# One Sign for two steps of a ternary weight, two row sums on another engine, and a new order of the preparation

## The reference, cut to what matters

```
x1 = x  + g * attention(layernorm(x), context)        Wq, Wkv, Wout; 8 heads, 128 context rows
x2 = x1 + g * W_proj' relu(W_fc' n + low-rank(n))^2   W' = ternary values times a scale per row
x3 = x2 + g * (Wx n + Wc mean(context) + b)           one matrix (512, 1024), split in two
x4 = x3 + g * (w2' q(gelu(w1' q(n) + b1)) + b2)       w' = ternary values times one scale; q: 8 bits
```

## Time and profile before

| what | value |
|---|---|
| runs, us | 1144.89, 1142.49, 1146.16 (median 1144.89) |
| the profiled execution's own time | 1145.46 |
| its span, first to last instruction | 1143.4 |
| TensorE, matmuls | busy 1086.2 (95%) |
| VectorE | busy 923.9 (81%) |
| ScalarE | busy 798.3 (70%) |
| POOL | busy 584.6 (51%) |
| mean granted clock of TensorE | 0.980 |
| moved by DMA | 128.11 MB |

### The profile page before, as it was taken

How to read it: one execution, slowest core, us unless ns; L and a number is a source line. 1 busy time by engine, 2 the same in 40 slices (tenths; PEclk the granted TensorE clock), 3 DMA queues, 4 the chain that set the end, 5 groups by cost and what they waited for, 6 DMA issues and landing times.

```text
span 1143.4 us, 22172 instructions
## 1 busy us (share of the span) xinstructions
PE 1086.2 (95%) x8270; PEld 676.6 (59%) x8558; DVE 923.9 (81%) x1989; ACT 798.3 (70%) x1575; POOL 584.6 (51%) x567
## 2 busy tenths in 40 slices
PE   5776799999999999999999999999999999999997
PEld 5544556475756656474756656565756666564744
DVE  3786788988788797878889888888878777988676
ACT  3988957677685949485876849495775868595634
POOL 1442646564655655556546457463546466564421
PEclk9988799999999999999999999999999999999998
DMA  9779751452534443433335245334343254333110
GB/s 335 239 241 317 232 147 41 95 130 65 120 79 103 98 105 86 100 82 87 93 83 139 61 112 97 86 101 87 89 99 99 54 109 114 75 93 74 38 47 28
DMA packets 273802, 128.11 MB, mean 112 GB/s; under 512 B 247568, under 2 KB 248080, under 8 KB 272016
## 3 DMA queue, kind: packets, MB, share of 16 engines
q1 hardware_dynamic: 273136, 125.73, 43.6%
q10 hardware_dynamic: 560, 0.96, 0.3%
HBM read 57.19 MB, written 8.39 MB: 57 GB/s over the span
## 4 chain that ended last, share of the span: by engine, by line
PE 86%; DMA 4%; ACT 3%; DVE 3%; issue 1%; SPq 1%; POOL 1%; ACTq 0%; DVEq 0%
PE ps L1844 19%; PE ps L1818 18%; PE ps L1887 10%; PE ps L1903 9%; PE ps L1866 7%; PE ps L1771 6%; PE ps L1718 6%; PE ps L1824 2%; PE ps L1758 2%; PE ps L1743 2%; DMA w1T<-in_wcT 1%; PE ps L1611 1%; DMA hT<-q 1%; PE ps L1683 1%; PE ps L1660 1%
## 5 line engine op out<-in xcount | busy, mean ns | idle before, releaser
L1818 PE MATMUL ps<-xT,fcT 128*128 128x256 f16 x2048 | 259.1, 274 | 8.2 <-DMA xT<-x16f 3.9
L732 POOL TENSOR_TENSOR rs<-ve,nhalf 128x1 f32<-128x1 f32 x160 | 102.1, 643 | 283.1 <-DVE ve L1357 207.9
L1844 PE MATMUL ps<-pjT,hid 128*128 128x512 fp8e4 x1024 | 232.1, 379 | 0.0
L1818 PEld LDWEIGHTS ps<-xT,fcT 128*128 128x128 fp8e4 x2048 | 199.1, 98 | 47.1 <-issue 6.5
L759 POOL TENSOR_TENSOR hid<-sq,hid 128x512 f16<-128x512 f32 x128 | 158.6, 1246 | 49.8 <-ACT sq L996 49.3
L1844 PEld LDWEIGHTS ps<-pjT,hid 128*128 128x128 f16 x1024 | 98.3, 98 | 98.9
L949 ACT ACTIVATE e<-ps,nmb,sig 128x128 f32<-128x128 f32 x256 | 113.0, 458 | 7.9 <-DVE nmb L1395 7.8
L985 ACT ACTIVATE rl<-ps,rsf 128x256 f32<-128x256 f32 x256 | 106.5, 469 | 15.6 <-PE ps L1824 14.9
L1887 PE MATMUL ps<-w1T,q4T 128*128 128x512 fp8e4 x480 | 113.4, 379 | 0.0
L764 POOL TENSOR_TENSOR e<-e,einv 128x512 f32<-128x512 f32 x64 | 71.0, 1116 | 74.2 <-DVE einv L1399 73.9
L1903 PE MATMUL ps<-w2T,hT 128*128 128x512 fp8e4 x480 | 108.6, 379 | 0.3 <-DMA hT<-q 0.3
(11 more groups left out here) (243 smaller groups left out, 1987.6 us busy)
## 6 DMA issues: line engine op xcount, KB each, us to landing
xb<-in_x SPq DMA_DIRECT2D x16, 512.0 KB, 4.3
xa<-in_x SPq DMA_DIRECT2D x15, 512.0 KB, 3.9
out<-r SPq DMA_DIRECT2D x30, 256.0 KB, 2.3
rope<-in_rope SPq DMA_DIRECT2D x16, 384.0 KB, 3.5
h<-in_w1T SPq DMA_DIRECT2D x6, 1024.0 KB, 6.4
h<-in_w2T SPq DMA_DIRECT2D x6, 1024.0 KB, 5.9
hid<-in_w_fc SPq DMA_DIRECT2D x2, 1024.0 KB, 8.7
h<-in_wkvT SPq DMA_DIRECT2D x2, 1024.0 KB, 10.3
```

The source lines that it names most:

```text
L732: pool.tensor_tensor(rs[:, n, t:t + 1], ve[:, n, t:t + 1], nhalf[:, :], ALU.pow).then_inc(done, 1)
L1818: pe.matmul(ps[:, FFN0 + m % 2, a * G:(a + 1) * G], fcT[:, k, f * P:(f + 1) * P], xT2[:, xs, k, :], start=(xs == 0 and k == 0), stop=False)
L1844: mm = pe.matmul(ps[:, FFN0 + t, :], hid[:, xs, c, t * P:(t + 1) * P], pjT[:, c, :], start=(c == 0 and xs == 0), stop=(c == FC - 1 and xs ...
```

## The change

1. The lift and the clip of w1 and w2 become one ScalarE operation, Sign with bias -MAGIC, from the rounded piece straight to fp8 in w1T or w2T. The clips, their two buffers and the constant go; c_tern12 counts in the place of c_lift and c_clip. The waits for the free destination (wc used for w1T, wx's two halves made for w2T) move from VectorE to ScalarE.
2. `ROWS_ACT = 2`: the row sums of w_fc's pieces 2 and 3 are made by VectorE, one reduce over (4, 512) each, inside "thr 2" and "thr 3".
3. ORDER and PREP are set anew. In groups 2 to 15 the positions shift, and the sequences on each engine differ from before by an operation passing a few neighbours, some of them in nearly every group. In the preparation and the first two groups they differ by more, as below.

```diff
+        ROWS_ACT = 2
...
-                dve.wait_ge(c_rows, KC * (i + 1))
...
+                if q < ROWS_ACT:
                     dve.wait_ge(c_rows, KC * (i + 1))
                 else:
-                    sc, cols = scd[:, i:i + 1], slice(FC + i, FC + i + 1)
                     arrived(dve, q)
-                    dve.tensor_reduce(sc, piece[PLACE[q]], axis=AX.X, op=ALU.add, apply_absolute_value=True).then_inc(c_rowd, 1)
-                    dve.wait_ge(c_rowd, i + 1)
+                    dve.tensor_reduce(sc, src, axis=AX.X, op=ALU.add, apply_absolute_value=True).then_inc(c_rowd, 1)
+                    dve.wait_ge(c_rowd, q - ROWS_ACT + 1)
...
                     act.wait_ge(c_round, n + 1)
-                    if n >= 2:
-                        act.wait_ge(c_clip, n - 1)
-                    else:
-                        used(act, last_in(4))
-                    act.activation(lifted[n % 2], piece[PLACE[W0 + n]], ACT.Relu, bias=lift[:, :]).then_inc(c_lift, 1)
+                    act.activation(dst, piece[PLACE[W0 + n]], ACT.Sign, bias=drop[:, :], saturate=False).then_inc(c_tern12, 1)
...
-            def clip_weights(n):
...
                 if first(g) and u == 0:
-                    pe.wait_ge(c_clip, 4)
+                    pe.wait_ge(c_tern12, 4)
```

More of the change, by code:

```diff
@@ L241, in build @@
         ktmp = rl[:, :, :]
-        lifted = [hT[:, t, :, :].rearrange("p c n -> p (c n)").bitcast(BF16) for t in range(TILES)]
         vT_sb = small[:, 0:KC * RANK].rearrange("p (k r) -> p k r", k=KC)
@@ L529, in build @@
-        PREP = dict(
-            PE=dict(x3_turn=(632, 634), q4_turn=(638, 642), q5_turn=(648, 649, 650, 651, 653, 654, 655, 656),
-                    k=(2, 3), v=(5, 6), low=(0,), mix=(14,), tern=(4, 9, 11, 16, 18, 19, 20, 21), low_t=(23,),
-                    row_scale=(27,), mean=(30,), spread=(1, 10, 12, 15, 26)),
-            DVE=dict(x3lo_end=(814, 817), ctx_sum=(14,), rot_k=(8, 9), wq_max=(4,), wq_scale=(5,), k_max=(16,),
-                     wq_lo=(7,), v_max=(17,), kv_scale=(23,), k_lo=(27,), v_lo=(31, 36), low_copy=(22,),
-                     thr=(6, 13, 18, 34, 44, 45, 47, 48), wo_max=(20,), v_top=(24,), wo_scale=(25,), wo_lo=(29,),
-                     mix_row=(51,), low_rank=(39,), v_parts=(52,), wx_max=(50,), hidden=(55,), wx_scale=(67,),
-                     wx_lo=(88,), row_scale=(62,), mean=(70,), diag=(56,), round=(72, 73, 81, 86, 90, 91, 98, 102),
-                     clip=(76, 80, 87, 92, 94, 97, 114, 129)),
-            ACT=dict(q4_end=(549, 550), wq=(5,), k_hi=(18,), v_hi=(20, 21), tanh=(1,), wo=(19,),
-                     evac=(7, 14, 16, 30, 34, 35, 36, 37), rows=(4, 8, 10, 22), whole=(6, 11, 13, 29), low=(42,),
-                     wx=(53,), sums=(39, 40, 41, 44, 45, 46, 47, 49), lift=(55, 56, 64, 67, 74, 79, 81, 83)),
-            POOL=dict(whole=(19, 20, 21, 22), rot_k=(7, 8), csb=(13,), low_zero=(14,)),
-            SP=dict(u=(1,), rows=(15,), ctx=(0,), wk=(4,), wq=(2,), wv=(7,),
-                    piece=(3, 5, 9, 16, 14, 22, 21, 18, 26, 28, 30, 31, 32, 35, 36, 37, 38, 39, 43, 44, 46, 49, 52, 55),
-                    wo=(8,), wc=(20,), wx=(19,), b1=(45,)))
@@ new lines, in build @@
+                pv=((17, 22), (47, 52), (84, 87), (122, 123), (160, 162), (198, 201), (237, 241), (272, 278),
+                    (314, 316), (354, 357), (395, 396), (434, 435), (466, 475), (511, 515), (549, 553), (588, 592)),
+                wo=((24, 25), (54, 55), (89, 90), (125, 126), (166, 167), (203, 204), (243, 244), (282, 283),
+                    (319, 320), (359, 360), (399, 400), (438, 439), (478, 479), (518, 519), (557, 558), (594, 595)),
+                low=((33,), (60,), (95,), (133,), (174,), (211,), (251,), (289,), (330,), (370,), (408,), (447,),
+                     (486,), (524,), (564,), (603,)),
@@ new lines, in build @@
+        PREP = dict(
+            PE=dict(x3_turn=(632, 634), q4_turn=(638, 641), q5_turn=(648, 649, 650, 651, 653, 654, 655, 656),
+                    k=(1, 2), v=(6, 7), low=(12,), mix=(14,), tern=(4, 8, 10, 16, 18, 19, 20, 21), low_t=(23,),
+                    row_scale=(26,), mean=(30,), spread=(0, 9, 11, 15, 29)),
+            DVE=dict(x3lo_end=(806, 808), ctx_sum=(6,), rot_k=(7, 10), wq_max=(0,), wq_scale=(3,), k_max=(19,),
+                     wq_lo=(8,), v_max=(20,), kv_scale=(23,), k_lo=(26,), v_lo=(28, 32), low_copy=(29,),
+                     thr=(9, 16, 17, 38, 44, 45, 46, 48), wo_max=(21,), v_top=(22,), wo_scale=(24,), wo_lo=(30,),
+                     mix_row=(50,), low_rank=(40,), v_parts=(70,), wx_max=(55,), hidden=(51,), wx_scale=(66,),
+                     wx_lo=(81,), row_scale=(63,), mean=(68,), diag=(52,), round=(69, 73, 78, 83, 86, 87, 93, 107)),
+            ACT=dict(q4_end=(547, 548), wq=(4,), k_hi=(16,), v_hi=(17, 20), tanh=(1,), wo=(19,),
+                     evac=(7, 13, 14, 28, 32, 33, 34, 35), rows=(5, 8), whole=(6, 11, 12, 27), low=(38,), wx=(50,),
+                     sums=(37, 39, 40, 41, 42, 45, 46, 49), lift=(52, 57, 61, 66, 70, 79, 83, 87)),
+            POOL=dict(whole=(19, 20, 21, 22), rot_k=(6, 7), csb=(9,), low_zero=(14,)),
+            SP=dict(u=(3,), rows=(25,), ctx=(0,), wk=(2,), wq=(1,), wv=(5,),
+                    piece=(4, 9, 11, 16, 18, 13, 17, 21, 26, 27, 31, 30, 34, 35, 36, 37, 38, 41, 42, 43, 44, 49, 50, 56),
+                    wo=(12,), wc=(14,), wx=(20,), b1=(45,)))
@@ L1287, in prepare @@
                     dve.tensor_copy(lowsb, lowprod).then_inc(c_low, 1)
-                for n in here("DVE", "clip", p):
-                    clip_weights(n)
                 for n in here("DVE", "round", p):
```

286 lines of the change are left out of this document (140 added, 146 removed), and 126 rows, old and new, of tables (down, exp, h, hid).

## The result

The changed kernel takes **1150.3 us** (median of 6 runs, 1147.53 to 1151.52), the kernel before 1145.21 in the same session (6 runs): the ratio is 1.0050, 95% interval 1.0037 to 1.0063. It is slower by half a per cent, 5.7 us by the ratio. The forecast was 1140.4, with a range up to 1145.5; the slower rival, C, had been given 0.07 and a mechanism that did not come about. Later comparisons are given as ratios to the kernel before in the same session, which there had medians of 1143.92 to 1144.72; 0.1% is 1.1 us.

A forecast was written before the change was run, and what follows sets the result against it. The preparation before TensorE's dense part at about 145 us was taken as the bound; the profiled 1145.46 less 4.5 gave 1141.0, and the median of runs, 0.57 lower, 1140.4 us, with a range of 1134.5 to 1145.5.

The forecast's parts named there:

- Rival C: Slower: VectorE's reduce delays low_rank, spread 3 and later ternary pieces; 2.5 to 4.5 us lost, 1147 to 1149; chance 0.07.
- (1) Eight clips: Eight clips leave VectorE, 13.1 us; first needed far behind 145 us, so worth nothing alone, only freeing VectorE's queue.
- Later orders: Orders behind the first groups differ by swaps of neighbours under a dense TensorE: 0, with 1.5 us either way.
- The walk: Step-by-step forecast of the preparation up to group 1's output projection, 4 to 4.5 us gained by then.
- Start: wq issued 0.5 us earlier, low-rank product no longer first: K starts at 14.2 us, before at 17.71.
- The low-rank product: Moved behind ternary piece 2, priced at 6.98 us, running to 52; scores then start at 52.4, 0.9 us gained.
- The mix: After group 0's scores: with the gap filled it costs 6.9 us instead of 10.16, ending at 64 instead of 71.1.
- w_proj: POOL's first rounding at 73.1 to 73.4, four pieces at 2.9 us each and a pv give 86: 1.5 us gained.
- Mean: Loads and ScalarE's sums for group 1: mean at 107.9 us for 110.50, 2.6 us gained.
- first up: First up product at 111.2 us for 119.52, its activation on ScalarE at 125.0 for 129.18: 4.2 us gained.
- Rival A: Loads before the mean bind, so only ScalarE's shorter list counts: 1 to 3 us gained, 1142 to 1144; chance 0.25.
- Rival B: Scores and low_rank come further forward, mix's 3.3 us also collected: 8 to 11 us, 1134 to 1137; chance 0.28.

The follow-up runs named there:

- e8: Kernel before with its orders and row sums, eight Signs replacing lifts and clips of w1 and w2, addresses kept by a spare tile: ratio 1.0002 to the kernel before.
- e1: Changed kernel with an unused tile where the constant lift was, so all later tiles keep their old addresses: 1143.12 us, ratio 0.9992 to the kernel before.
- e9: Changed kernel with the spare tile, its own orders up to group 3's second value product, then the kernel before's on all queues: 1140.22 us, 0.33% under the kernel before.
- e7: Kernel before's preparation with one Sign for lift and clip, the change's orders from group 2's ups, addresses aligned: ratio 1.0071 to the kernel before.
- e11: Changed kernel with the spare tile, low-rank product back at the head of TensorE's queue: ratio 1.0079 to the kernel before.

## Why the prediction was wrong

Two steps failed, and both were priced at nothing.

**"(1) Eight clips ... are worth nothing by themselves."** Right of the clips (e8). But the same edit takes the constant `lift` away, and the prediction gave its removal no price. By the addresses it moved, it cost 6.6 us (1.0050 less 0.9992), more than the whole forecast gain. The addresses could be worked out from the list of tiles. Among the rivals there was none for it.

**"Later orders differ by swaps of neighbours under a dense TensorE: 0, with 1.5 either way as the bound."** They cost 2.9 us by e1 less e9 and 7.9 by e7 less e8, both outside the bound. The stage is dense, but 98.6% dense: waits of 0.3 to 2.2 us each, the scores' for the low halves of q above all, come in with these orders, and a few of them in a thousand microseconds are enough. A bound for them wanted the slack between producer and consumer at each swapped place.

From the kernel before to the changed one by way of e9 and e1: -3.8, +2.9 and +6.6, +5.7 in all. The three add up by construction and are no check of one another.

**The walk** itself, point by point:

- Start: K at 13.81 (14.2 forecast). Right.
- The low-rank product took 3.74 at its new place, not the 6.98 that it was priced at. At the head of the queue it takes 6.98 and 7.00 (e11).
- The mix took 9.34, not 6.9: the granted clock was 0.62 in 50 to 60. In e1, with the same orders, it took 7.10 and TensorE idled 4.0 behind it, as the walk had both. It was not on the path in either, since low_rank ended at 64.07 (67.6 forecast; 12.8 behind the scores' end, where the walk had 12.5).
- w_proj: POOL's first rounding ended at 69.44 (73.1 forecast). The four pieces went at the walk's 2.9 each (69.50 to 81.02), but the second value product then waited 2.06 for the last p's transposes and ended at 83.92 (86). In the chain of waits stand VectorE's four reduces with a p_lo between, and 6.64 us for those transposes.
- Mean 107.01 (107.9), first up 110.55 (111.2), activation 123.36 (125.0), downs 137.76 (140). Right to about 2 us, early throughout. The mean's lead came by other terms than forecast: the loads of w2 stand with 11.27 us in its chain, where the walk had ScalarE's list alone.

Rival A's mechanism shows: ScalarE idles 1.5, 0.8 and 0.7 for w2 ahead of its sums, 3.0 in all, and without it the mean would have come up to as much earlier. Rival B's came about for the scores and low_rank, 3.9 and 3.5 us earlier than forecast, of which 2.1 were left at the second value product and 0.9 at the mean. Rival C did not come about. The loss came from two places that no rival named.

## What to carry to other kernels

When an edit adds or drops a tile, however small, list the addresses of all tiles behind it before pricing anything else, and keep what a DMA transpose reads at multiples of 256 bytes; comparing one kind's landing medians between two profiles shows a slip at once. When an edit brings new orders, try the early and the late part alone, with a seam at one moment on all queues: a good preparation and a bad tail hide one another. And before a row's duration is used at another place, ask at which clock it ran.
